# Score and value products of a linear attention on four 64x64 array tiles, by renaming the slots of a token-major layout

## The reference, cut to what matters

```python
def step(S, inp):
    r_t, dec_t, k_t, v_t, kk_t, a_t = inp
    b_t = kk_t * a_t
    sa = jnp.einsum('bvk,bk->bv', S, -kk_t)
    S = S * dec_t[:, None, :] + sa[:, :, None] * b_t[:, None, :] + v_t[:, :, None] * k_t[:, None, :]
    o_t = jnp.einsum('bvk,bk->bv', S, r_t)
    return (S, o_t)
```

## Time and profile before

| | |
|---|---|
| median of 3 runs | 310.4 us (310.08 to 311.84) |
| the profiled execution | 311.29 us |
| its span | 309.4 us |
| mean granted TensorE clock | 0.982 of full |
| PE / PEld busy | 91% / 70% of the span, 5976 records each |
| DVE / ACT / POOL busy | 60% / 65% / 41% |
| mean duration of one PE record | 0.196 us (109*45 109x18), 0.207 (128*45 128x45), 0.201 (64*45 64x45), 0.220 (128*45 128x64), 0.321 (128*64 128x180), 0.325 (64*64 64x180) |
| the chain that ended last | PE 67%, ACT 19%, DVE 7%, POOL 3%, issue 2% |

### The profile page before, as it was taken

The page is one execution under the profiler, slowest core; times in us unless marked ns, Lnnn a source line. Parts: engine busy times, 40 slices in busy tenths (PEclk is TensorE's granted clock), DMA queues, the critical chain, the costliest instruction groups (busy, mean ns, idle before and its releaser), DMA issues.

```text
span 309.4 us, 13783 instructions
## 1 busy us (share of the span) xinstructions
PE 282.9 (91%) x5976; PEld 217.7 (70%) x5976; DVE 186.6 (60%) x337; ACT 199.8 (65%) x356; POOL 127.0 (41%) x122
## 2 busy tenths in 40 slices
PE   3999599999989999999878976999999999999996
PEld 1567487888966676767554464888899888976785
DVE  5459858899395872434636979689765664244202
ACT  1787964555574878887898886194875325666541
POOL 9016999022050057576436049684388200021000
PEclk9999979999995999999999999999999999999999
DMA  7932212222222222222200000000000000000002
GB/s 235 393 97 61 63 56 65 61 61 63 55 62 59 60 61 58 59 62 61 61 28 2 0 2 2 4 4 5 4 4 4 4 4 5 4 2 2 2 28 74
DMA packets 20564, 15.01 MB, mean 49 GB/s; under 512 B 2328, under 2 KB 19352, under 8 KB 20376
## 3 DMA queue, kind: packets, MB, share of 16 engines
q1 hardware_dynamic: 20504, 14.13, 14.8%
HBM read 13.38 MB, written 0.74 MB: 46 GB/s over the span
## 4 chain that ended last, share of the span: by engine, by line
PE 67%; ACT 19%; DVE 7%; POOL 3%; issue 2%; DVEq 0%; POOLq 0%
PE PS L781 62%; PE PS L898 5%; ACT L343 3%; ACT arena L373 2%; ACT arena L369 2%; ACT arena L367 2%; ACT arena L408 2%; DVE K L555 1%; DVE PS L511 1%; ACT arena L416 1%; ACT arena L382 1%; DVE arena L679 1%; ACT arena L420 1%; POOL arena L327 1%; POOL arena L322 1%
## 5 line engine op out<-in xcount | busy, mean ns | idle before, releaser
L781 PE MATMUL PS<-arena,K 64*64 64x180 f32 (+3 forms) x1392 | 133.3, 364 | 13.8 <-DVE PS L511 5.3
L781 PEld LDWEIGHTS PS<-arena,K 64*64 64x64 f32 (+2 forms) x1392 | 77.5, 143 | 53.0 <-issue 18.1
L781 PE MATMUL PS<-arena 128*45 128x45 f32 (+5 forms) x3584 | 106.9, 222 | 4.4 <-POOL arena L316 2.3
L781 PEld LDWEIGHTS PS<-arena 128*45 128x45 f32 (+3 forms) x3584 | 97.7, 124 | 18.0 <-issue 5.8
L306 POOL TENSOR_TENSOR arena<-arena 128x360 f32<-128x360 f32 x32 | 29.9, 961 | 35.4 <-DVE arena L693 35.2
L693 DVE TENSOR_TENSOR arena<-PS,arena 128x360 f32<-128x360 f32 x32 | 16.8, 530 | 24.1 <-PE PS L781 20.0
L282 POOL TENSOR_TENSOR WG<-WG,K 128x2048 f32<-128x2048 f32 x4 | 15.3, 3835 | 29.9 <-DMA WG<-wr 29.9
L408 ACT ACTIVATE arena<-PS,K 128x720 f32<-128x720 f32 x32 | 25.2, 861 | 2.1 <-PE PS L781 1.5
L390 ACT COPY arena<-PS 128x720 f32<-128x720 f32 x16 | 12.4, 775 | 17.0 <-PE PS L898 16.8
L781 PE MATMUL PS<-K,arena 128*45 128x64 f32 (+4 forms) x472 | 19.2, 231 | 2.8 <-DVE arena L568 1.4
L781 PEld LDWEIGHTS PS<-K,arena 128*45 128x45 f32 (+3 forms) x472 | 17.5, 129 | 5.0 <-issue 2.4
(11 more groups left out here) (126 smaller groups left out, 372.3 us busy)
## 6 DMA issues: line engine op xcount, KB each, us to landing
WG<-wr SPq DMA_DIRECT2D x64, 64.0 KB, 1.9
arena<-wr SPq DMA_DIRECT2D x64, 64.0 KB, 1.8
arena<-xT SPq DMA_DIRECT2D x4, 368.0 KB, 5.5
K<-consts SPq DMA_DIRECT2D x1, 1171.0 KB, 11.4
K<-consts SPq DMA_DIRECT2D x1, 852.0 KB, 9.2
out<-arena SPq DMA_DIRECT2D x4, 180.0 KB, 1.9
K<-consts SPq DMA_DIRECT2D x1, 510.0 KB, 7.7
K<-consts SPq DMA_DIRECT2D x1, 352.0 KB, 7.7
```

What stands on the lines that cost most here:

```text
L781: return nc.tensor.matmul(o, l, r, start=start, stop=stop)
```

## The change

A new function `held(s, h)` says which sequence (as a slot of the feature-major layout and its half) lies in slot s and half h of the token-major layout. Before, slot p and half j of one layout were slot p and half j of the other. Now slot 4i + 2j + m and half h of the token-major layout hold the sequence of slot 4i + 2m + h and half j of the feature-major one (i, j, m, h are 0 or 1). So source half j and destination half h take all four combinations.

- `m`: the loops run over m, the three products, and the four (j, h). The matmul reads partition half j and writes half h of bank j. The number and the shapes are as before: 24 matmuls in each `m`.
- `vt`: 16 matmuls, but over 64 rows, with the 64x64 block of `Wvf` that isn't zero. The row tile decides the bank: 256 columns in each of the two banks instead of 512 in bank 0. ScalarE's two copies read `both(c, 256)`.
- `o`: the same 32 matmuls on two column tiles; weights and moving operand come from the renamed slot, and the output goes to the slot of the feature-major layout.
- Nothing else changes: the steps between work on each (slot, half) alone, and TABLE, the waits and the sizes of all arrays stay.

```diff
-                        last = s.activation(a(c, VT_[j], 512), bank(c, 0, 512), ACT.Copy, scale=vec(f"tok{j}"))
+                        last = s.activation(halves(a(c, VT_[j], 512)), both(c, 256), ACT.Copy, scale=vec(f"tok{j}"))
...
+            def held(s, h):
+
+                i, j, m = s // PH, s % PH // 2, s % 2
+                return PH * i + 2 * m + h, j
...
-                    for q in range(PP // 2):
-                        p = i * PP // 2 + q
+                    for m in range(2):
                         for u in range(3):
-                            for j in range(2):
+                            for j, h in quads:
+                                p, _ = held(PH * i + 2 * j + m, h)
                                 kt, bt, kr1 = [half(c, at + p * T, j, 0, T, 64) for at in (slot(7), slot(5), KR_ + p * T)]
                                 kr2 = half(c, KR_ + 2 * p * T, j, 0, 2 * T, 64)
                                 l, r = [(kt, kr2), (bt, kr2), (kr1, bt)][u]
-                                col = (q % 2) * 5 * T + 2 * T * u
-                                last = mm(PS[64 * j:64 * j + T, 2 * c + q // 2, col:col + (1 if u == 2 else 2) * T], l, r)
+                                col = m * 5 * T + 2 * T * u
+                                last = mm(PS[64 * h:64 * h + T, 2 * c + j, col:col + (1 if u == 2 else 2) * T], l, r)
...
-                    for p, j in pairs:
-                        last = mm(to_bank(c, 0, D, j, p, T), a(c, slot(6) + at(p, j), T),
-                                  k("Wvf", 64 * (p // PH), 64 * (p // PH) + 64))
+                    for q in range(PH):
+                        for row, h in quads:
+                            p0, p1 = 64 * row, 64 * row + 64
+                            p, j = held(PH * row + q, h)
+                            last = mm(PS[64 * h:64 * h + T, 2 * c + row, D * q:D * q + D],
+                                      a(c, slot(6) + at(p, j), T, p0, p1), k("Wvf", p0, p1, p0, p1))
...
-                    for p in range(PP):
-                        for u in range(2):
-                            for j in range(2):
-                                last = mm(bank(c, 0, T, p * T, 64 * j, 64 * j + 64),
-                                          a(c, (SA_, VT_)[u][j] + p * D, D), m4(c, p, (3, 1)[u]), start=(u == 0),
-                                          stop=(u == 1))
+                    for q in range(0, PP, PH):
+                        for m in range(2):
+                            for h in range(2):
+                                for u in range(2):
+                                    for j in range(2):
+                                        slot_ = q + 2 * j + m
+                                        p, _ = held(slot_, h)
+                                        last = mm(bank(c, 0, T, p * T, 64 * j, 64 * j + 64),
+                                                  a(c, (SA_, VT_)[u][h] + slot_ * D, D), m4(c, slot_, (3, 1)[u]),
+                                                  start=(u == 0), stop=(u == 1))
```

## The result

The changed kernel takes 309.32 us (median of 15 runs, 308.63 to 313.86), the kernel before 310.42 us beside it. The ratio is 0.996, 95% interval 0.9941 to 0.9978: 1.2 us faster, 0.7 to 1.8. The forecast was 2.7 us, 307.7.

The account below looks back on a forecast made before the run. TensorE, busy 91% of the span with 67% of the chain, was taken as the bound. Terms 0.95 + 1.4 + 1.6 = 3.9 us, cut to 2.7 by instruction supply, took 310.4 to 307.7 us; range 306.2 to 309.9.

Parts of the forecast that it names:

- Price of a step: On four tiles time per record halves: `m` to 16.8 ns, saving 0.80 us; `vt` to 14.2 ns, saving 0.45 us.
- Rival 2: Weight loads or instruction issue hold short matmuls at 21.5 ns a record: 308.4 us, chance 0.15.
- Before 192.8 us: 0.: Chunk 0's `m` and `vt.0:0` lie under a GpSimd run that doesn't wait for them: 0 saved for the end.
- rival 5: Emptier TensorE loses clock: a 6.8 us fall in full work costs 3.4 us, 311.1 us; chance with rival 4, 0.08.
- First term, 0.95 us: From 192.8 us, chunk 1's `m` and `vt` let ScalarE's part of the chain start 0.95 us earlier.
- the lead at 211 us: Sign of being wrong: the changed kernel's lead at 211 us isn't near 0.95 us.
- the fall of the clock: Sign of being wrong: TensorE's granted clock falls in the changed kernel.
- Second term, 1.4 us: From 211.93 us, chunk 2's two `m` give 1.60 us, less about 0.2 waiting for VectorE; `vt.0:2` is lost.
- Third term, 1.6 us: Chunk 3's `m.0:3` and `m.1:3` save 1.6 us; `vt.0:3` is lost to a wait for VectorE.
- the second limit: From 210.2 to 264.35 us instruction packets, one in 3.73 us, could hold the whole saving to 2.1 us.
- the cut: Instruction supply lowers the summed saving of 3.9 us to 2.7 us.
- rival 4: From 210 us every instruction block lasts 3.96 us: 1.2 us slower, 311.6 us; chance with rival 5, 0.08.

Follow-up runs that it names:

- e8: Changed kernel with `vt` on two array tiles again, `m` still on four: 308.82 us, ratio 0.9968 to the kernel before.
- e9: Changed kernel with GpSimd's addition L282 moved from step `lx.0` to step `w`: 309.10 us, ratio 0.996 to the kernel before.
- at `w`: GpSimd's addition L282 moved to step `w`, in the kernel before (311.75 us) and in the changed kernel (309.10 us).
- the pair behind `m.1:3`: All four GpSimd additions L282 moved behind step `m.1:3`, in the kernel before (310.98 us) and in the changed kernel (312.10 us).
- e2: Changed kernel with 45 instead of 64 moving columns in `u`, `y2`, `z`, `w`, as many instructions: 307.98 us, ratio 0.9923 to the kernel before.
- e13: Changed kernel with GpSimd's addition L282 moved from step `lx.0` to step `u.0`: 310.61 us, ratio 1.0008 to the kernel before.
- e16: Changed kernel with all four GpSimd additions L282 moved behind step `m.1:3`: 312.10 us, ratio 1.0024 to the kernel before.
- e12: Kernel before with GpSimd's addition L282 moved from step `lx.0` to step `w`: 311.75 us, ratio 1.0043 to the kernel before unmoved.

## Why the prediction was wrong, step by step

- **Price of a step.** Right: 17.0 and 14.2 ns a record (16.8 and 14.2 forecast); `vt` brings nothing that can be measured (e8). Rival 2 is out. The rule of the Trainium skill, "TensorEngine Tiling (Array Packing)", section Performance Considerations, on dimensions that are already small would, as the prediction reads it, have left `vt` and the 45-column third of `m` unchanged; the measurement decides against it.
- **Before 192.8 us: 0.** Right only where the clock holds. `m.0:1` came 0.55 us late by its fall, rival 5 in kind. The prediction had priced a fall of 6.8 us in full work at 3.4; the one that came lasted 3.4 us and cost 0.55 us there. It cost nothing more at the end only because the collision would have taken the same time.
- **First term, 0.95 us.** The step that failed: the mask behind the scan "comes only 0.8 to 0.95 us earlier". The term measured 0.35 us. ScalarE's part did start at 201.89, where 202.0 was forecast, but that is luck: 0.69 us of it was there before any changed step, and the change's own share is 0.35. The prediction followed the scan's inputs and not the engine beside it. Either the clock's fall or GpSimd's L327 holds it, and they don't add. With both away the term is 1.05 to 1.07. Two of the prediction's own signs of being wrong had come: the lead at 211 us, and the fall of the clock.
- **Second term, 1.4 us.** Right: 1.33 from `m.0:2` to `lx.0:2` (1.68 less 0.35), 1.33 in e9.
- **Third term, 1.6 us, and the second limit.** The right mechanism. After has 0.75 us of it at `o.0:0` (2.43 less 1.68) and then loses 0.65 to 250 us; the cut was sized at 1.2 us for the whole, the profile shows 1.5: 3.9 less the 0.6 of the first term is 3.3, and 1.8 remain. How much of the 1.5 is supply alone isn't shown: the gaps of after are 0.8 us longer than those of before. Supply as a hard limit from 210 us on (rival 4) didn't come: 128 matmuls pass in 3.4 to 3.7 us, not 3.96.
- **The sum.** 2.7 less 0.6 (first term) less 0.3 (the third cut, larger than forecast) is 1.8 us, the lead in the profiles; the timed 1.2 us (0.7 to 1.8) includes it only at its edge, and the rest is open.

How far the collision is shown: in the profiles directly (the same scan at 196.84 and 196.65 us, with and without GpSimd beside it), and by the leads at `m.0:2` of the runs with L282 elsewhere. Each is of one execution, but they repeat within 0.02 us. The timed pairs lean the same way, 2.6 us at `w` against 1.2, but their intervals touch, and the pair behind `m.1:3` shows that a gain can be turned around by where the next collision falls.

## What to carry to other kernels

Before a saving on one engine is counted, look at what the other engines are doing at the new time of each step behind it, VectorE with both inputs in SBUF beside GpSimd above all: tenths of a microsecond in the start decided over 0.6 to 3.3 us. The trace of the kernel before can warn of it: an instruction of one line and one shape that takes 1.4 us in some places and 0.91 in others asks what runs beside it. A long GpSimd operation with time to spare belongs where no such VectorE step is near. In dense runs of short matmuls count instructions, not only nanoseconds: near 128 matmuls in 3.4 to 3.7 us, less work turned into gaps here (e2).

## What the runs showed of the hardware

- How much VectorE loses beside GpSimd: an operation on SBUF alone went from 0.91 to 1.54 us (L706 beside a GpSimd operation of 0.89), from 0.49 to 3.32 and 3.77 (L768), from 0.52 to 2.99 (L726) and from 0.59 to 3.36 (L576) beside one of 3.82; it ended 0.3 to 0.8 us behind the other.
- Four 64x64 tiles take fp32 matmuls of 45 to 90 columns at 17.0 and 14.2 ns a record, half of the 33.6 and 28.4 with two tiles at a time.
- The clock fell to 0.50 for 3.4 us in a stretch that the change had made emptier (1.42 us busy in the 4.2 before it); faster work on TensorE can cost clock. It fell to 0.50 near 180 or 189 us in all ten profiles with chunk 0 on four tiles and in none of the ten with two. It fell once more behind single long waits of TensorE, of 2.7 us in e13 and 3.0 us in e16.
- The supply of instructions isn't one rate: 11 packets came from 224 to 265 us in before, after and e12, of 0.95 to 1.2 us each, and the gaps from 212 to 272 us sum to between 0.3 us (e12) and 3.4 (e2).
